# Half of the output projection ahead of the third scores, and its residual behind the first tile's sum

## What is computed

```python
def attention(x):                      # x is layer-normed
    xx = shifted(x) - x
    r, k, v = ((x + xx * maa) @ W.T for r, k, v)   # 32 heads of 16 channels
    g = silu((x + xx * maa_g) @ Wg.T)
    # chunks of Q = 64 tokens, a scan over the chunks of a sequence:
    att = rc @ kc * w_mat              # scores of a chunk, weighed by the decay
    yc = att @ vc + rc @ state * wb    # own chunk, and product with the state
    state = ws * state + kc * wk @ vc
    yn = groupnorm(y, by head) * gamma + beta
    return yn * g @ Wo.T               # the output projection
x = x + attention(layernorm(x))        # the residual
x = x + ffn(layernorm(x))              # 512 -> 2048, gelu, -> 512
```

## Time and profile before

| | us |
|---|---|
| median of 3 executions | 2078.05 (2074.58 to 2080.48) |
| the profiled execution, its own time | 2075.69 |
| its span, from first to last instruction | 2073.9 |
| busy: PE / PEld | 2002.3 / 1423.9 |
| busy: DVE / ACT / POOL | 1738.2 / 1293.5 / 317.5 |
| mean granted clock of TensorE | 0.994 |
| DMA engines, mean | 228 GB/s |

### The profile page before, as it was taken

One profiled execution on the slowest core, in us unless ns is written; L12 is line 12 of the kernel. 1 busy time (PEld: TensorE's weight loads), 2 busy tenths in 40 slices (PEclk: granted clock), 3 DMA queues, 4 the chain that ended last, 5 costly groups with the idle time before them and its releaser, 6 DMA issues.

```text
span 2073.9 us, 64752 instructions
## 1 busy us (share of the span) xinstructions
PE 2002.3 (97%) x27206; PEld 1423.9 (69%) x27206; DVE 1738.2 (84%) x3687; ACT 1293.5 (62%) x2081; POOL 317.5 (15%) x329
## 2 busy tenths in 40 slices
PE   5889999999999999999999999999999999999999
PEld 5777667667666767766766776676776667667666
DVE  7778889888888988888988888898888888888761
ACT  7876565676566666655657765666765656666452
POOL 1111111111111111111111111111111111111110
PEclk8999999999999999999999999999999999999999
DMA  6977677888777788777778877778887877887777
GB/s 214 220 199 237 177 236 216 248 239 233 200 233 220 236 241 241 213 226 227 230 231 245 248 203 225 234 215 247 250 231 202 231 220 230 250 238 203 216 249 250
DMA packets 428979, 471.97 MB, mean 228 GB/s; under 512 B 259600, under 2 KB 309392, under 8 KB 428688
## 3 DMA queue, kind: packets, MB, share of 16 engines
q1 hardware_dynamic: 427056, 467.64, 77.2%
q10 hardware_dynamic: 1632, 0.18, 0.1%
HBM read 316.21 MB, written 25.17 MB: 165 GB/s over the span
## 4 chain that ended last, share of the span: by engine, by line
PE 81%; DMA 4%; SPq 4%; DVE 3%; ACT 3%; issue 3%; POOL 0%; ACTq 0%; DVEq 0%
PE F L1132 20%; PE F L1068 17%; PE B L879 10%; PE B L1040 8%; PE sc L879 7%; PE YT L911 6%; PE YT L879 3%; PE YT L963 2%; DMA y<-ygT 2%; PE sc L941 2%; PE YT L982 2%; DMA ring<-w_dram 1%; SPq L2027 1%; PE YT L1012 1%; PE F L836 1%
## 5 line engine op out<-in xcount | busy, mean ns | idle before, releaser
L1132 PE MATMUL F<-ring,hT 128*128 128x512 f16 x1984 | 467.5, 379 | 0.0
L1068 PE MATMUL F<-xT,ring 128*128 128x256 f16 x3840 | 449.3, 273 | 5.1 <-ACT hT L1768 3.7
L1068 PEld LDWEIGHTS F<-xT,ring 128*128 128x128 f16 x3840 | 369.8, 98 | 64.9 <-issue 8.0
L1132 PEld LDWEIGHTS F<-ring,hT 128*128 128x128 f16 x1984 | 189.1, 98 | 197.9 <-issue 0.5
L879 PE MATMUL B<-mix,WT 128*128 128x256 f16 x2304 | 267.5, 273 | 0.4 <-DVE gT L1372 0.3
L1768 ACT ACTIVATE hT<-F,b,f_rho 128x256 f16<-128x256 f32 x480 | 243.5, 560 | 37.9 <-PE F L1068 37.9
L879 PEld LDWEIGHTS B<-mix,WT 128*128 128x128 f16 x2304 | 222.6, 98 | 33.8 <-DVE gT L1372 0.6
L276 DVE SCALAR_TENSOR_TENSOR mixf<-dx,maa,xnT 128x256 f32<-128x256 f32 x512 | 238.6, 526 | 0.1
L1725 ACT ACTIVATE Shl<-S 128x256 f16<-128x256 f32 x128 | 53.1, 415 | 263.7 <-PE YT L982 148.6
L1971 POOL TENSOR_TENSOR Shl<-S,Shl 128x256 f16<-128x256 f32 x128 | 89.2, 697 | 734.7 <-ACT Shl L1725 734.7
L1719 ACT ACTIVATE att<-att 128x512 f16<-128x512 f32 x256 | 147.5, 624 | 68.3 <-DVE att L1333 68.3
(11 more groups left out here) (196 smaller groups left out, 2997.6 us busy)
## 6 DMA issues: line engine op xcount, KB each, us to landing
ring<-w_dram SPq DMA_DIRECT2D x512, 512.0 KB, 4.6
kx<-kT SPq DMA_DIRECT2D x96, 256.0 KB, 3.8
rx<-rT SPq DMA_DIRECT2D x96, 256.0 KB, 4.4
xa<-in_L_attn_x SPq DMA_DIRECT2D x32, 512.0 KB, 7.6
vbd<-vN SPq DMA_DIRECT2D x256, 64.0 KB, 3.1
x<-in_L_attn_x SPq DMA_DIRECT2D x32, 512.0 KB, 6.1
out<-x SPq DMA_DIRECT2D x31, 512.0 KB, 3.8
w_dram<-ring SPq DMA_DIRECT2D x20, 256.0 KB, 3.8
```

Source lines behind the costliest of these rows:

```text
L1068: mm = eng.matmul(up_place(f, j)[:, i * BT:(i + 1) * BT], ring[:, use % RING, i, a * C + kk * P:a * C + (kk + 1) * P], xT[:, :, kk, :], st ...
L1132: mm = eng.matmul(F[:, t, :], hT[:, k, rows(t)], ring[:, use % RING, i, a * C:(a + 1) * C], start=(k == 0 and a == 0), stop=(k == NH - 1 a ...
```

## The change

In `pe_step` the first half of the output projection is put between the products with the state and the third chunk's scores; the two pieces of weight preparation (which do nothing but in steps 0 and 1) stay behind the scores. In `dve_steady` the residual of the first tile is taken directly behind `dve_take_y(n, 0)`, and the gate ahead of the low part of the mix. `dve_step`, with the order of the steps 0 to 2, is as it was. No wait is added or removed.

```diff
@@ -1233,10 +1233,11 @@
             pe_up(eng, n, 7)
         if att_n:
             pe_from_state(eng, n, 0)
+        if tail:
+            pe_Wo(eng, n, 0)
+        if att_n:
             pe_scores(eng, n, 2)
             pe_prepare(eng, n, "sc2")
-        if tail:
-            pe_Wo(eng, n, 0)
             pe_prepare(eng, n, "Wo0")
         if ff:
             pe_down(eng, n - 2, 0)
@@ -1478,16 +1479,16 @@
         dve_gated(eng, n - 1)
         dve_weights_lo(eng, n, 1)
         dve_state(eng, n, 1)
+        dve_gate(eng, n, 1)
         if ahead:
             mix_lo(eng, n + 1, 0)
-        dve_gate(eng, n, 1)
         dve_take_y(eng, n, 0)
+        dve_residual(eng, n - 1, 0)
         dve_weigh(eng, n, 2)
         if ahead:
             mix_lo(eng, n + 1, 1)
         dve_weights_lo(eng, n, 2)
         dve_variance(eng, n, 0)
-        dve_residual(eng, n - 1, 0)
         dve_state(eng, n, 2)
         dve_weigh(eng, n, 3)
         dve_weights_lo(eng, n, 3)
```

## The result

The change takes 2091.84 us (median of 4 runs, 2089.84 to 2095.87) against 2076.32 us for the kernel before in the same batch (4 runs, 2072.64 to 2080.48). The ratio is 1.0073, 95% interval 1.0056 to 1.0089: **slower by 0.7%**, where the forecast was 2066.5 us and faster. The profiled execution took 2095.87 us, its span 2094.1, which is 20.2 longer than that of before; it is the slowest of its four, and the medians differ by 15.5.

The account below looks back on a forecast made before the run. PE, busy 97% of the span, was taken as the bound, waiting at times for its next 256 instructions; -16.0 - 3.4 + 5.9 + 1.0 + 1.2 = -11.3 us gave 2066.5 us, range 2059 to 2078 (8 in 10).

Parts of the forecast that it names:

- Step (1): PE's waits for code in third and fourth scores and output projection mostly vanish: -16.0 us, bounds 0 and -19.3.
- step (4): VectorE's residual waits 0.57 us for the projection; second values products keep 0.25 us free: +1.0 us, bounds 0 and 5.8.
- Rival B: Half of PE's waits come back elsewhere and VectorE's thin slack is missed in most steps: about 2078 us, chance 0.18.
- Step (2): Two half-clock stretches on PE behind long waits in the third scores go: -3.4 us, bound 0.
- Step (3): More switches on PE between array quarters and whole array: 0.19 us in 31 steps, +5.9 us, bounds 5.6 and 10.
- Step (5): VectorE's gate ahead of the mix's low part waits 0.25 us for ScalarE's tanh, covered by idle: cost 0.
- Step (6): In step 1 the second weight preparation piece waits for ScalarE's copy of the first: +1.2 us, bounds 0 and 2.5.
- A: PE's waits follow the place behind the dense attention block, not the instruction count: +8.1 us, 2086, chance 0.10.
- C: The change only moves a hidden release, of B, leaving only the switches' +5.9 us: 2084, chance 0.02.
- if PE's second values product shows a wait in every step: Named sign, in PE's timeline at the second products with the values, that the forecast is wrong.

Follow-up runs that it names:

- e8: e3 with VectorE's gate put back behind the low part of the first mix, as in the kernel before: 2072.51 us, 0.9972 of the kernel before.
- e3: The change, with the low part of the next block's second mix moved on VectorE behind the fourth chunk's update: 2070.41 us, 0.9962 of the kernel before.
- e12: The change with 12 more short products (24 records) on PE, once, in front of step 3's first scores: 2087.18 us, 1.0044 of the kernel before.
- e1: The change's new order on PE with VectorE's old order: 2082.76 us, 1.0032 of the kernel before.
- e9: e3 with the first chunk's variance on VectorE also moved behind the fourth chunk: 2072.53 us, 0.9971 of the kernel before.
- e10: e9 with the mask of the fourth chunk also ahead of its low weights on VectorE: 2067.66 us, 0.9949 of the kernel before.
- e11: The change with the mask of the fourth chunk ahead of its low weights on VectorE: 2081.83 us, 1.0012 of the kernel before.

## Why the prediction was wrong

**Step (1), the waits given back, is the first that failed.** The waits of the third scores (excess 12.7 to 0.3) and of the projection (3.9 with the clock to 0.4) went as said; those at the first state products mostly stayed (5.3 from start to start, now 3.6), as said. What failed is "Sum -16.0" as a balance: it treated each packet alone. A PE that no longer stands in the third scores reaches the second values products sooner against VectorE (in these five steps VectorE's release led by 1.15 to 1.94 us before and by 0.10 to 0.16 after, of which step (4) accounts for 0.6), and there the request of a packet is held back (the table of requests). Steps 9, 14, 19, 24 and 29, which lost a wait in the third scores, got one of 2.2 to 3.3 at their end: 13.5 us, and steps 8 and 13 got 1.6 more at their start. Rival B had this ("half of the waits come back elsewhere") but looked behind the scores, at small ones. The sum of a removed wait is not known until one has said where the engine stands next.

**Step (4), VectorE, is the second.** The residual's wait was forecast as 0.57 and is 0.51; "done near 1016.84" for the low weights was right too. But the text took them for the last thing that the second values products wait for. They also wait for the mask of the fourth chunk (`s_km` in `pe_att_v`), queued directly behind, with this row in the kernel before:

```profile
1016.19 0.48 DVE L1352 SCALAR_TENSOR_TENSOR kv<-YT,flag,headmask 128x256 f32<-128x256 f32 x1
```

It ended at 1016.67, not at 1016.27. With 0.57 more that is 1017.24, and the products, which without it would have started at 1017.09, start about 0.1 behind it: 0.25 late in each of 29 steps, 7 us. Measured: 5.8. The forecast took +1.0 and named 5.8 as its bound. And it priced the miss as a delay alone; that a late request leaves later still behind a late release was in no term. The table shows it: with PE's order and stops the same, the five waits fall from 13.5 to 3.9 us when the release leads by 0.70.

**Step (2), the clock**, followed from (1): -3.4 forecast. The stretch at 209 and that at 1861 are gone, but four in the steady steps (3.4, 6.8, 6.8 and 3.4 us long, with 18.5 us of PE's busy time in them, so 9.2 lost) came instead: +5.8.

**Step (3), the switches**, was right: +0.19 forecast, +0.17 in step 15, and 2.8 + 2.6 - 0.6 = 4.8 us over 28 steps, 0.17 each. The larger bound, a whole drain at both ends, did not come true. The Trainium skill's rule that changing the tiling mode drains the TensorE (TensorEngine Tiling (Array Packing), Key Properties) fits in kind, with 0.10 and 0.09 us at the two borders here; a whole drain is not shown.

**Step (5), the gate**: 0 forecast; e8 against e3 shows no difference. **Step (6), step 1's preparation**: +1.2 forecast, and PE waits 1.21 us for ScalarE in front of the second piece:

```profile
157.36 1.13 PE L836 MATMUL F<-xT,hT 128*128 128x128 f32 x8 [1.21 <-ACT hT L851]
```

All the steps ahead of the steady ones took 1.5 more. The change did not make them: step 1's state products, ahead of which it touches nothing, started at 150.03 instead of 147.09, and 1.4 of these 2.9 us came back by step 3.

**Slips in the working**, none of which moved the forecast: in (1) the lower bound is -19.1 by its own terms and not -19.3. In (4) the weighing starts 1.3 later and not 0.7, since the residual takes 0.74 itself, which leaves the fourth scores 0.4 and not 0.5. And 25 waits in a step would give a drift of 3 records in five steps; with 24 it is the 8 that the rows show.

**The rivals.** A (the waits follow the place, 2086) falls: those in the scores are gone, and e12 moves waits with 24 records. Its number is nearer to the measured time, for the wrong reason. C (a hidden release, 2084) falls with them. B named both parts of what happened and priced each too low. Of the text's own signs of an error, "if PE's second values product shows a wait in every step" is the one that came true, in 20 of the 29 steps.

Two things stay open. The table shows that the release sets the time of a late request; why the same packets were requested ahead of it in the kernel before, and behind it with the change, is not shown. That PE came to the wait later against VectorE is no full answer: in e1 it came there nearly as early as in the change, after a stop for the residual, and the requests left in time. And e9 and e10 took 2 to 3 us out of the five waits against e3 without a shorter span. In the steady steps they got back 2.5 and 3.2 us behind the gate's projection, mostly waits for ScalarE, and e10 2.7 in the first state products; what ties these to the rest is open.

The ISA Cache section of the Trainium skill (Advanced Engine Details and Errata) gives lines of 256 instructions and two of them; e12 agrees with the 256, and a packet that is fetched while the one before it runs agrees with the two. Its 128 KB for TensorE, by which rival A would have held, would be eight such lines, an estimate from its two figures. That this is more than a step's instructions says nothing, since the program is written out and no step's code runs twice; but PE stood 2.2 to 3.3 us for the very next packet, so no look-ahead of that depth shows here.

## What to carry to other kernels

A wait that is removed on the bounding engine moves that engine ahead of all the others: before counting it as a gain, walk on to its next semaphore and list every wait there, with the last operation that each depends on and its slack. Where waits for code show, give the releases near them a lead: here a lead of 0.10 us went with 13.5 us of such waits in five steps, 0.70 with 3.9 and 1.55 with 1.1. One 1.2 us operation, moved on VectorE to where nobody waits for it, turned a loss of 0.7% into a gain of 0.4%.

## What was unexpected of the hardware

- The request for the next packet of code can follow the release of a semaphore for which the engine waits: in the change, e11, e3, e9 and e10 it left 1.0 to 1.5 us behind a release with a lead of 0.48 or more, and up to 2.9 behind one with 0.10 (table above). In the kernel before and in e1 most requests were ahead of the release. The transfer looked at took about 0.9 us (19.3% of 16 engines in a stretch of 0.3), and PE goes on 2.2 to 3.0 us behind its start.
- The length of a wait does not decide on the clock by itself. In e11 the waits of 1.65 and 1.96 us were followed by a granted clock near one half, the one of 2.52 was not (stretches directly behind the three, columns as in the earlier trace rows):

```profile
653.60:657.00 3.40, 3.40 (x12) 1.47 (x11) 3.30 (x6) 1.05 (x2) 0.67 (x1) 0.59 0.02 5
961.60:965.00 3.40, 3.38 (x15) 1.30 (x15) 2.88 (x6) 1.05 (x2) 0.67 (x1) 0.53 0.03 6
1269.30:1272.70 3.40, 3.15 (x23) 2.04 (x23) 2.79 (x5) 1.04 (x2) 0.67 (x1) 1.00 0.11 20
```

- Code that does nothing moved the waits: the 24 records of e12 moved the borders of packets, and with them the long waits, to other steps. The ratio went from 1.0073 to 1.0044, but the intervals of the two overlap slightly, so that a gain in time is not shown.
